# A fused graph attention and mixture-of-experts kernel: the order of its setup changed, and the first projection tiles moved beside the last attention units

## The reference

```python
# layer 1, on layernorm(x): 16 heads of width 32
seq = (x @ W_seq).reshape(N, H, DH)
score1 = einsum('nhd,d->hn', seq, a1); score2 = einsum('nhd,d->hn', seq, a2)
scores = leaky_relu(score1[:, :, None] + score2[:, None, :], 0.2) + (1.0 - adj) * -65500.0
hidden = einsum('hij,jhd->ihd', softmax(scores, -1), seq).reshape(N, D_IN)
x = x + elu(hidden @ W_out + b_out)
# layer 2, on layernorm(x): a shared two-layer net (512 -> 2048 -> 512, squared relu) plus
# two of eight experts for each row, behind a down-projection to 256 (fc1) and an up-projection (fc2)
x = x + ffn(layernorm(x))
```

## Time and profile before

| | us |
|---|---|
| three runs: median (lowest to highest) | 1066.85 (1062.9 to 1067.52) |
| the profiled execution: its own time | 1063.74 |
| its span, first to last instruction | 1061.9 |
| busy: TensorE / VectorE / ScalarE / GpSimd | 1003.7 / 801.6 / 666.4 / 247.5 |
| mean granted clock of TensorE | 0.981 |

### The profile page before, as it was taken

How to read it: one execution, slowest core, us unless ns; L and a number is a source line. 1 busy time by engine, 2 the same in 40 slices (tenths; PEclk the granted TensorE clock), 3 DMA queues, 4 the chain that set the end, 5 groups by cost and what they waited for, 6 DMA issues and landing times.

```text
span 1061.9 us, 27192 instructions
## 1 busy us (share of the span) xinstructions
PE 1003.7 (95%) x11256; PEld 889.3 (84%) x11256; DVE 801.6 (75%) x1197; ACT 666.4 (63%) x990; POOL 247.5 (23%) x271
## 2 busy tenths in 40 slices
PE   4993989999999999997999999999999999999998
PEld 4872889999999999996777888888888877878887
DVE  5666999999999999973799533448675569976554
ACT  1568999999999898940556433334445546655441
POOL 0101024433433344343332000000075000006500
PEclk9996989999999999998999999999999999999999
DMA  8485111111111111533636000020063124453242
GB/s 300 140 287 173 42 61 43 42 43 62 42 42 57 48 42 43 203 97 115 229 114 210 16 1 1 1 80 1 1 222 121 55 70 126 131 168 114 85 134 99
DMA packets 53762, 102.45 MB, mean 96 GB/s; under 512 B 6145, under 2 KB 26241, under 8 KB 53122
## 3 DMA queue, kind: packets, MB, share of 16 engines
q1 hardware_dynamic: 47218, 82.73, 23.4%
q10 hardware_dynamic: 3360, 9.67, 2.6%
q0 software_dynamic: 3072, 8.39, 2.4%
HBM read 74.69 MB, written 26.08 MB: 95 GB/s over the span
## 4 chain that ended last, share of the span: by engine, by line
PE 48%; issue 2%; DVE 2%; DMA 1%; POOL 0%; ACT 0%; SPq 0%; POOLq 0%; DVEq 0%; ACTq 0%
PE bank L1253 16%; PE bank L1720 16%; PE bank L1085 3%; PE bank L1797 2%; PE bank L1748 1%; PE bank L1749 1%; PE bank L1751 1%; DMA xs<-sorted_latent_rows 1%; PE bank L1767 1%; PE bank L1705 1%; PE bank L1741 1%; PE bank L1082 1%; PE bank L1703 1%; PE bank L1073 1%; PE bank L1094 1%
## 5 line engine op out<-in xcount | busy, mean ns | idle before, releaser
L665 ACT ACTIVATE arena<-arena 128x1024 fp8e4<-128x1024 f32 x320 | 336.4, 1135 | 2.5 <-ACT arena L657 1.4
L874 PE MATMUL bank<-arena 128*128 128x132 f16 x4096 | 285.1, 221 | 29.4 <-DVE arena L738 18.3
L874 PEld LDWEIGHTS bank<-arena 128*128 128x128 fp8e4 x4096 | 246.2, 98 | 31.3 <-issue 19.5
L1253 PE MATMUL bank<-xt,up_parts 128*128 128x512 f32 x768 | 186.3, 391 | 0.0
L1720 PE MATMUL bank<-down_parts,h_parts 128*128 128x512 f32 x768 | 184.4, 389 | 0.0
L878 PE MATMUL bank<-arena 128*128 128x66 f16 x4096 | 172.9, 196 | 0.0
L1720 PEld LDWEIGHTS bank<-down_parts,h_parts 128*128 128x128 f32 x768 | 143.9, 188 | 30.1 <-issue 0.2
L1253 PEld LDWEIGHTS bank<-xt,up_parts 128*128 128x128 f32 x768 | 142.3, 188 | 28.7 <-ACT relu_sb L1202 0.2
L723 DVE TENSOR_SCALAR arena<-arena 128x1024 uint8<-128x1024 f32 x192 | 166.2, 932 | 0.0
L878 PEld LDWEIGHTS bank<-arena 128*128 128x128 fp8e4 x4096 | 154.3, 98 | 0.1
L1227 DVE TENSOR_TENSOR relu_sb<-relu_sb 128x512 f32<-128x512 f32 x64 | 44.2, 691 | 118.5 <-ACT relu_sb L1202 114.7
(11 more groups left out here) (231 smaller groups left out, 1398.8 us busy)
## 6 DMA issues: line engine op xcount, KB each, us to landing
hid<-in_adjT SPq DMA_DIRECT2D x32, 512.0 KB, 5.7
arena<-s_rows SPq DMA_DIRECT2D x30, 512.0 KB, 3.5
sorted_latent_rows<-zeros SPq DMA_DIRECT2D x1, 4992.0 KB, 18.3
xs<-sorted_latent_rows SPq DMA_DIRECT2D x39, 128.0 KB, 2.2
sorted_expert_rows<-expert_y SPq DMA_DIRECT2D x39, 128.0 KB, 1.7
arena<-in_x SPq DMA_DIRECT2D x4, 1024.0 KB, 11.4
xr<-in_x SPq DMA_DIRECT2D x16, 256.0 KB, 2.8
up_sb<-in_upT ACTq DMA_DIRECT2D x1, 4096.0 KB, 14.4
```

What stands on the lines that cost most here:

```text
L665: last = nc.scalar.activation(m8[:, k, j, :], s1b[:, k % 2, :], ACT.Sigmoid, bias=bias_now[:, k % 2, j:j + 1], scale=STEEP, saturate=False)
L874: last = nc.tensor.matmul(o, m8[:, k, j, i * P:(i + 1) * P], vs[:, b, j, :], start=(j == 0), stop=(j == T - 1))
L1253: last = nc.tensor.matmul(bank[6 + s % 2][:, :], sa[:, s % 2, a, k, :], xt[c][:, b, k, :], start=(i == 0), stop=(i == len(mm) - 1))
```

## The change

In setup: the constants are issued by SyncE ahead of W, W is loaded in two halves, the transposes of x use three banks and are grouped in threes, project(0) stands ahead of score_columns, the orders of ScalarE and VectorE are rewritten (casts earlier, any_neighbour ahead of natural_scores, any_neighbour(1) ahead of mask_acts(0, 0)), and degrees(1) stands ahead of unit 0. At the end of attention: half of the reciprocals, split_low, normalise of tiles 0 to 2, the transposes and copies of tiles 0 and 1 are put beside units 30 and 31 (in banks 6 and 7), and the projection of tile 0 stands in the first block behind unit 31.

```diff
+        X_BANK = [bank[0], bank[1], bank[5]]
-        WA_BANK = bank[3]
+        WA_BANK = bank[7]
-        ROW_BANK = [bank[4], bank[7], bank[5], bank[6]]
+        ROW_BANK = [bank[4], bank[5], bank[0], bank[1]]
         def setup_loads(sp):
-            sp.dma_start(wt_sb, w_seqT.rearrange("(c p) k -> p c k", p=P)).then_inc(wt_loaded, 16)
+            sp.dma_start(ident, ident_in[:, :]).then_inc(consts_loaded, 16)
+            sp.dma_start(a_cols_sb, a_cols[:, :]).then_inc(consts_loaded, 16)
+            sp.dma_start(a_mask_sb.rearrange("p c h -> p (c h)"), a_mask[:, :]).then_inc(consts_loaded, 16)
+            for c in range(2):
+                sp.dma_start(wt_sb[:, 2 * c:2 * c + 2, :], w_seqT[c * 2 * P:(c + 1) * 2 * P, :].rearrange("(c p) k -> p c k", p=P)
+                             ).then_inc(wt_loaded[c], 16)
         # setup_act
-            for s in range(8):
-                copy_v(s)
-                if s < 7:
-                    high_x(2 * s + 2, 2 * s + 3)
-                if s % 2:
-                    copy_scores(s // 2)
-                if s >= 2:
-                    cast(2 * s - 3)
-            cast(13)
-            copy_v(8)
-            cast(15)
-            copy_v(9)
+            cast(1)
+            copy_v(1)
+            high_x(4, 5, 6)
+            copy_scores(0)
+            cast(3)
+            copy_v(2)
+            high_x(7, 8, 9)
+            cast(5, 7)
+            copy_v(3)
+            high_x(10, 11, 12)
+            copy_scores(1)
+            cast(9)
+            copy_v(4)
+            high_x(13, 14, 15)
+            copy_scores(2)
+            cast(11)
+            copy_v(5)
+            copy_scores(3)
+            cast(13, 15)
+            copy_v(6)
             cast(17)
-            copy_v(10)
-            cast(19)
+            copy_v(7)
...
             act.dma_start(s1_dram[:, :], s1_rows).then_inc(s1_stored, 16)
+            cast(19)
+            copy_v(8)
+            cast(21)
+            act.wait_ge(s1_stored, 16)
+            for k in range(2):
+                act.dma_start(s1b[:, k, :], s1_dram[k:k + 1, 0:IC].to_broadcast([P, IC])).then_inc(s1_staged[k], 16)
+            copy_v(9)
             act.wait_ge(expin_ready, 1)
...
+            cast(23)
+            copy_v(10)
+            cast(25)
         # setup_dve
+            nc.vector.memset(wa.bitcast(f32), 0.0)
+            centre_w()
             diagonal_a()
-            centre_w()
...
-            cast(10, 12, 14)
-            natural_scores()
-            cast(16)
-            any_neighbour(0)
+            cast(10)
+            bound_factor()
+            cast(12, 14)
+            any_neighbour(0)
+            natural_scores()
+            cast(16, 18)
             exponents()
-            cast(18)
+            cast(20)
             apply_empty_rows((0,))
-            cast(20)
+            cast(22)
             apply_empty_rows((1,))
-            cast(22)
+            cast(24)
             scale_columns()
         # setup_pe
             transpose(0, 1)
+            pe.wait_ge(w_ready, 1)
+            project(0)
+            transpose(2, 3)
             score_columns()
+            project(1)
+            transpose(4, 5, 6)
+            scores(0)
...
+            project(6)
             scores_to_tokens()
+            project(7)
             scores_to_rows()
             degrees(0)
+            project(8, 9, 10, 11, 12, 13, 14, 15)
+            degrees(1)
         # scalar, first block
-                copy_v(13)
-                cast(25)
+                cast(27)
+                copy_v(11)
+                cast(29)
                 act.wait_ge(bias_copied, 1)
                 act.wait_ge(s1_staged[0], 16)
-                compare_rows(0, DVE_J, DVE_J + 2)
+                compare_rows(0, DVE_J, DVE_J + 1)
+                copy_v(12)
+                compare_rows(0, DVE_J + 1, DVE_J + 2)
+                cast(31)
+                copy_v(13)
+                compare_rows(0, DVE_J + 2, DVE_J + 4)
                 copy_v(14)
-                cast(27)
-                compare_rows(0, DVE_J + 2, DVE_J + 4)
+                compare_rows(0, DVE_J + 4, DVE_J + 6)
                 copy_v(15)
-                cast(29)
-                compare_rows(0, DVE_J + 4, DVE_J + 6)
+                compare_rows(0, DVE_J + 6, DVE_J + 9)
                 split_high(0, 0)
-                compare_rows(0, DVE_J + 6, T)
-                cast(31)
+                compare_rows(0, DVE_J + 9, T)
...
+                act.wait_ge(wo_low, 1)
+                copy_h(act, 0)
+                copy_h(act, 1)
         # vector, first block
+                        if last and k == 2:
+                            dve.wait_ge(sums_free, UNITS)
+                            nc.vector.reciprocal(rden[:, 0:IT, :], hid[:, 0:IT, :, DH]).then_inc(rden_ready, 1)
+                            split_low()
                         if last and k == 3:
-                            split_low()
+                            low_of_h(dve, 0)
+                            low_of_h(dve, 1)
...
-                cast(24, 26)
+                cast(26)
                 mask_own(0, 0)
-                cast(28)
+                cast(28, 30)
+                any_neighbour(1)
                 low_values(0, 0)
                 mask_acts(0, 0)
-                cast(30)
                 dve.wait_ge(seq_in_psum, T)
                 compare(0, 1)
                 mask_own(0, 1)
-                any_neighbour(1)
         # gpsimd, first block
+                combine(PAIRS - 1, 0)
+                combine(PAIRS - 1, 1)
+                normalise(pool, 0)
+                normalise(pool, 1)
+                combine(PAIRS - 1, 2)
+                normalise(pool, 2)
+                combine(PAIRS - 1, 3)
         # tensor, first block
+                        if p == PAIRS - 1 and k == 3:
+                            pe.wait_ge(c2_loaded, 48)
+                            transpose_h(pe, 0)
+                            transpose_h(pe, 1)
...
+                pe.wait_ge(wo_low, 1)
+                pe.wait_ge(sums_ready, UNITS + 1)
+                project_tile(pe, 0)
```

More of the change, by code:

```diff
@@ L504, in scores @@
                 pe.wait_ge(xl_ready, 4 * c + 4)
+                pe.wait_ge(wa_ready, 1)
                 if c >= 2:
@@ L542, in setup_pe @@
             transpose(0, 1)
+            pe.wait_ge(w_ready, 1)
+            project(0)
+            transpose(2, 3)
             score_columns()
-            pe.wait_ge(w_ready, 1)
-            for s in range(8):
-                project(s)
-                if s < 7:
-                    transpose(2 * s + 2, 2 * s + 3)
-                if s % 2:
-                    scores(s // 2)
-            project(8)
+            project(1)
+            transpose(4, 5, 6)
+            scores(0)
+            project(2)
+            transpose(7, 8, 9)
+            project(3)
+            transpose(10, 11, 12)
+            scores(1)
+            project(4)
+            transpose(13, 14, 15)
+            scores(2)
+            project(5)
+            scores(3)
+            project(6)
             scores_to_tokens()
-            project(9, 10)
+            project(7)
             scores_to_rows()
-            project(11)
             degrees(0)
-            project(12, 13, 14, 15)
-            return degrees
+            project(8, 9, 10, 11, 12, 13, 14, 15)
+            degrees(1)
         x1 = hid_t.rearrange("p (t c) -> p t c", t=T)[:, :, 0:D]
@@ L602, in build, with copy_h, normalise, low_of_h @@
             "x1_ready", "var2_ready", "std2_ready", "xn2_ready", "xt2_in_psum", "xth_copied", "xtl_ready"))
+        def copy_h(act, t):
+            act.wait_ge(ht_in_psum, t + 1)
+            if t >= 2:
+                act.wait_ge(y_in_psum, t - 1)
+            nc.scalar.copy(hT[:, t % 2, 0, :, :],
+                           bank[6 + t % 2][:, :].rearrange("p (k n) -> p k n", k=KD)).then_inc(ht_copied, 1)
+        def normalise(pool, t):
+            pool.wait_ge(rden_ready, 1 if t < IT else 2)
+            if t >= 2:
+                pool.wait_ge(ht_in_psum, t - 1)
+            nc.gpsimd.tensor_tensor(hn[:, t % 2, :].rearrange("p (h d) -> p h d", h=H), hid[:, t, :, 0:DH],
+                                    rden[:, t, :].rearrange("p (h o) -> p h o", o=1).to_broadcast([P, H, DH]),
+                                    ALU.mult).then_inc(hn_ready, 1)
+        def low_of_h(dve, t):
+            dve.wait_ge(ht_copied, t + 1)
+            nc.vector.tensor_tensor(hT[:, t % 2, 1, :, :], bank[6 + t % 2][:, :].rearrange("p (k n) -> p k n", k=KD),
+                                    hT[:, t % 2, 0, :, :].bitcast(f32), ALU.subtract).then_inc(ht_low, 1)
+        def transpose_h(pe, t):
+            pe.wait_ge(hn_ready, t + 1)
+            if t >= 2:
+                pe.wait_ge(ht_low, t - 1)
+            for k in range(KD):
+                last = nc.tensor.transpose(bank[6 + t % 2][:, k * P:(k + 1) * P], hn[:, t % 2, k * P:(k + 1) * P], ident2)
+            last.then_inc(ht_in_psum, 1)
```

(21 more changed lines are left out.)

119 lines of the change are left out of this document (34 added, 85 removed).

## The result

| us | before | after |
|---|---|---|
| median (lowest to highest), 6 runs each | 1066.26 (1062.9 to 1067.52) | 1060.20 (1055.38 to 1061.08) |
| span of the profiled execution | 1061.9 | 1058.9 |
| mean granted clock | 0.981 | 0.983 |

The ratio is 0.9935 (95% interval 0.9913 to 0.9957): faster by 6.1 us by the medians (6.9 by the ratio), where 16.6 were forecast, and outside the range of 1044 to 1057. The rest of this document is about the 10 us that are missing. Most of them are missing in one place.

What follows compares the result with a forecast made beforehand. TensorE was taken as the bound, with holes in setup and after attention's last unit. Gains of 5.9 + 2.2 + 8.7 - 0.2 = 16.6 us from the median 1066.85 gave 1050.2 us, range 1044 to 1057.

Steps and rivals of the forecast that it cites:

- reaches the end whole: TensorE full again behind 515 us, so gains in setup and after attention's last unit would reach the end undiminished.
- the joint: Passage from attention's last units to the first projection tiles; transposes of tile 4 forecast 8.7 us earlier.
- Term 3: End of attention into projection: transposes of tile 4 at 506.3 instead of 515.0, gain 8.7 us (bounds 7.0 to 9.8).
- The chain over ScalarE is what is late next: First projection tiles: ScalarE's chain sets tile 4's transposes at 506.3; TensorE's own path comes earlier.
- Term 4: Around unit 30: two GpSimd normalises beside the split end 0.2 us after the unit, -0.2 us (0 to -1.0).
- Term 1: End of setup: ScalarE's last compare before unit 0 complete at 95.3 instead of 101.2, gain 5.9 us.
- the walk: Setup's three engine queues followed node to node with profiled durations, giving 95.3 us for compare(0, 0) complete, before 101.2.
- From here ScalarE is not held again: End of setup: after transfer 31's cast at 84.2, ScalarE runs without waits to its last compare at 95.3.
- Term 2: First attention units: VectorE has less work, mask_acts(0, 1) follows mask_acts(0, 0) sooner, gain 2.2 us (bounds 0 and 4.3).
- (c): Attention's end pays less: normalises held longer, unit 31 or block's end waits; gain 13 to 16, 1052.5 us, chance 0.10.
- (f): Setup: new TensorE holes could leave its clock at 1.2 GHz, about 2.7 us more per tile; slower side, chance 0.03.

Runs made afterwards that it cites:

- the pieces: Weight loads (6 MB) cut into six spaced 1 MB pieces; here on the kernel with old setup and the change's end-of-attention half: 1055.61 us, ratio to before 0.9913.
- the late kernel: The changed kernel with both weight loads whole, but issued behind the elu of tile 3 instead of at the second block's start: 1054.93 us, ratio to before 0.9892.

## Why the prediction was wrong

**What bounds it, and that a gain "reaches the end whole".** This is the step that failed. TensorE was full behind 515 us, and from that I concluded that everything moves with it. The six MB of weights did not move with it: they start with the block, which came 3.4 earlier, while the tiles came up to 13.3 earlier. Before, the hole and the slow tiles had covered their drain. The prediction counted the issues of these loads (1.0 on ScalarE) and not the 23 us until the last of their bytes lands (491.8 to 515.0), nor who asks for a small load in that time. Taking the load away gave 7.8 by the medians, where the trace had 7.6 lost; spacing the bytes gave 8.0, and the spacing by itself, on the kernel before, nothing. That the wait for xr, beside this burst, took the joint's gain is shown. The share of the constants ahead of xr on SyncE's queue is not.

**Term 3** (8.7): right in size at tile 4 (8.74 in the trace) and with the pieces in place (8.9 at tiles 4 and 7). "The chain over ScalarE is what is late next" held up to there; after it the load of xr was next.

**Term 4** (-0.2): TensorE did not wait for normalise at unit 31. The two normalises took 4.42 beside the split, 4.6 was taken. The bound of 1.0 was never reached, since they were complete at 475.5, as unit 30 ended. The Trainium skill (SBUF — State Buffer, "Who interferes with whom") says that a VectorE instruction with both inputs in SBUF contends with a GpSimd instruction that reads SBUF, and that the shared ports are an exclusive lock. The trace agrees: the 4.42 are 2.1 alone (1.05 each) and 2.3 more, beside VectorE's subtraction of 2.23, and the 3.59 at setup's end is 1.07 alone and 2.5 more, beside a mask instruction of 2.82.

**Term 1** (5.9): 4.4 in the profiled pair. This difference scatters, since the start of unit 0 hangs on the adjacency transfers: the four profiles with the old setup order have it at 104.17, 105.37, 109.21 and 101.88, the ten with the new one between 97.65 and 101.02 with a mean of 99.9. The means differ by 5.2. So the term may have been a little too large, but the old order alone scatters by 7.3. Within the profiled execution the walk held up to transfer 31's cast (84.1, forecast 84.2), and mask_acts(0, 0) came 1.5 late. What failed there is "From here ScalarE is not held again": the matmuls of project(14), behind the hole of 3.4, ran at a granted clock of 0.50, and ScalarE waited 1.00 and 0.23 for the last two tiles. With copy_v(12) moved these two waits are gone, but no time is gained that can be told.

**Term 2** (2.2): measured 0.04. The walk placed GpSimd's product for unit 1 at its undisturbed duration (2.5) and so found no wait at split_high(0, 1). It runs beside VectorE's mask and compares, and takes 6.4 (96.96 to 103.3), where the same four operations took 2.4 before. The prediction had priced this contention at the joint and not here. Moving the split gave the distance back (11.48), and by the medians the time.

**Rivals.** None of them was this. (c) came nearest, a joint that pays less, but it named the normalises and the block's end, and its 3 us at most. The slower clock of (f) did appear, for about one tile each time: as a consequence of the wait for xr, where the tile behind it took 2.9 longer, and behind the hole before project(14), where it held ScalarE for 1.2.

**Sum.** By the traces at tile 7: setup 4.6 instead of 8.1, the joint 1.2 instead of 8.5, together 5.7; measured 6.1.

## What to carry to other kernels

When a stretch gets shorter, list the transfers that were running under it, and for each small load behind it ask how long before its use it is issued and how many bytes stand in front: here the lead was 5.5 us before and 5.6 after, but the load had moved from 16.9 to 7.0 us behind the issue of 6 MB that took 23 to land. Look also at what stands ahead of the load in its own queue: a constant of 20 KB took 13.0 us beside the burst. Large loads for a later stage belong between the steps, one piece at a time, even if the queue that issues them has room at the block's start. And where two engines are shown to slow each other in one place, price it in every place where the new order brings them together.

## What the runs showed of the hardware

A load of 256 KB issued by SyncE took 12.1 us while 6 MB issued by ScalarE were draining, and 2.8 otherwise. A load of 19.5 KB took 13.0 beside them, and 3.9 in the late kernel, where nothing large was in flight. The Trainium skill (DMA: Bandwidth & Descriptors, "Queues, rings and completion order") says that a DMA engine takes turns between queues, a whole packet at a time; by that rule a small load should not wait for all bytes of another queue. The trace agrees: from 498.8 to 506.3 the two queues moved 457 and 464 packets, and xr landed 4 us ahead of the last of the 6 MB. By the same count a queue of small packets beside one of large ones moves few bytes (0.08 MB beside 2.48), and what stands behind them in that queue waits.

After a hole of 3.4 (before project(14)) the matmuls of that tile ran 0.43 apart instead of 0.23, at a granted clock of 0.50 from 82.3 to 87.6.
